# Wide matmuls on a constant ahead of, and between, the first matmuls of an attention stage

## Chip, cores and metric

The kernel runs on one core of one Trainium2 chip. The metric is the device time of one execution in microseconds; the time before is the median of three runs. The profile is one further execution of the same kernel on the same core.

## The reference, cut to what matters

Two transformer layers over T = 1024 tokens of width C = 512, each an attention followed by a feed-forward part, with residuals and a layer norm behind each. Both attentions have 32 heads of width 16 over all 1024 tokens and are causal.

```python
q, k = rope(q), rope(k)
scores = einsum('bhqd,bhkd->bhqk', q, k) / sqrt(16)
attn = softmax(where(causal, scores, -inf))
y = einsum('bhqk,bhkd->bhqd', attn, v)
```

Layer 0 has a small adapter attention over ten extra tokens besides, then a lookup part as feed-forward. Layer 1 has eight key and value heads, each shared by four query heads, and a SwiGLU feed-forward. The change touches only the attention stage, which both layers run.

## The kernel before, in words

The stages follow one another with a barrier between them: projection of layer 0, adapter, attention 0, its finish, lookup, projection of layer 1, attention 1, its finish, SwiGLU. `attention(nc, layer, ...)` is built once for each layer.

An attention stage works in 16 units `u`: eight head groups `g` (four heads each) for the lower 512 queries (`c` = 0), then the same eight groups for the upper 512 queries (`c` = 1). I call the first eight the narrow units and the last eight the wide ones. A narrow unit has 4 key tiles `kt` of 128 keys, a wide one has 8.

For each unit the kernel does two things.

- *Maxima.* The row maxima of the scores must be known before the exponentials. `entry(number, b, what)` multiplies queries by keys (line 849, `q_st` as weights, 48 rows), adds the causal mask on the diagonal block with two bf16 matmuls on constants (lines 855 and 857, `picks` and `maskb`), and VectorE reduces the result (line 973). A narrow unit has 12 such entries, a wide one 28, and one more entry "T" (line 837) transposes the previous unit's maxima. Entries go round a ring of three PSUM banks (`RING`), so TensorE is at most three entries ahead of VectorE. GpSimd splits the maxima in two parts (lines 998 and 1000), VectorE joins their halves in wide units (line 948) and copies their transpose out of PSUM (line 964), and four small DMAs (line 810) write them as two extra rows into `q_st`.
- *Attention proper.* `scores(u, kt, p)` (line 872) computes transposed scores with the maximum already subtracted through the extra rows; it waits for those DMAs at the unit's first key tile and for the exponential two steps back. ScalarE takes the exponential (line 926), GpSimd masks the diagonal tile (line 1013), `values(u, kt)` (line 891) multiplies by the values into PSUM bank 6, and ScalarE copies the finished unit out (line 934).

The order on TensorE is written out by hand. First the entries of units 0 and 1 with nothing between them, then the two first `scores`, then the loop over units: in unit `u` the key tiles' `scores` and `values` are interleaved with the entries of unit `u + 2`, spread evenly over the unit's slots. So units 0 to 5 carry the entries of narrow units, units 6 and 7 carry the entries of wide units, units 8 to 13 are wide with wide entries, and units 14 and 15 have none. The last instruction of a unit shows in the trace as the copy of line 934, which ScalarE issues behind the second exponential of the next unit.

The DMA queue in layer 0 holds, when the stage begins, the loads of the first four units' queries and keys and behind them the 2 MB load of `x_tok` (line 602, issued in the adapter stage). In layer 1 only the first unit is loaded before the stage; units 1 to 3 are issued at its start.

The constant `picks[0]` is the 128x128 bf16 tile that the mask matmuls of line 855 also read. Bank 6 is not used before the first `values`, which starts a new accumulation.

Of the kernel before, what the change touches and what calls it, by code (L numbers as in the profile page):

```python
# [32 lines left out]
P = 128  # L33
# [705 lines left out]
def attention(nc, layer, phase, stacked, arena_o, arena_p, v_tok, v_grp, ident, picks, maskb, psum):  # L739
# [18 lines left out]
    def key_pair(p):  # L758
        return p if layer == 0 else 0
# [26 lines left out]
    def first_column(c, kt):  # L786

        return max(0, P * kt - 512 * c)

    with phase as ph, ExitStack() as own:  # L790
# [37 lines left out]
        def _(pe):  # L828
            def entry(number, b, what):

                if number >= len(RING):
                    pe.wait_ge(qk_taken, number - len(RING) + 1)
                bank = RING[number % len(RING)]
                if what == "T":
                    u = b - 1
                    pe.wait_ge(max_ready, u + 1)
                    pe.transpose(psum[0:2 * R * 4, bank, 0:P],
                                 mst[:, u % 2, :, :].bitcast(F32).rearrange("p j i -> p (j i)"), ident[:, :])\
                        .then_inc(qk_ready, 1)
                    return  # L840
                i, heads, kc, width = what
                s, c = b % NS, steps[b][0]
                if number == first_entry[b]:
                    pe.wait_ge(q_loaded[s], 32 * (b // NS + 1))
                    pe.wait_ge(k_loaded[s], 32 * (b // NS + 1))
                for n, r in enumerate(heads):
                    p, rows = r // 2, slice(64 * (r % 2), 64 * (r % 2) + KS)
                    end = width * (n + 1)
                    last = pe.matmul(psum[:, bank, width * n:end],  # L849
                                     q_st[rows, s, p, P * i:P * i + P],  # L850
                                     k_st[rows, s, key_pair(p), 512 * kc:512 * kc + width],
                                     start=True, stop=kc < c)
                    if kc == c:
                        half = slice(64 * (r % 2), 64 * (r % 2) + 64)
                        pe.matmul(psum[:, bank, end - P:end], picks[0][half, :], maskb[half, :],  # L855
                                  start=False, stop=False)
                        last = pe.matmul(psum[:, bank, end - 64:end], picks[1][half, :],  # L857
                                         maskb[half, 0:64], start=False, stop=True)
                last.then_inc(qk_ready, 1)

            def scores(u, kt, p):

                s, c = u % NS, steps[u][0]
                n = first_exp[u] + 2 * kt + p
                o = first_column(c, kt)
                if kt == 0 and p == 0:
                    pe.wait_ge(max_loaded[s], 64 * (u // NS + 1))
                if n >= 2:
                    pe.wait_ge(exp_ready, n - 1)
                for t in range(2):  # L870
                    rows = slice(64 * t, 64 * t + KM)
                    last = pe.matmul(psum[:, 2 * (n % 2) + t, o:512],  # L872
                                     k_st[rows, s, key_pair(p), P * kt:P * kt + P],
                                     q_st[rows, s, p, o:512], start=True, stop=True)
                last.then_inc(scores_ready, 1)

            def values(u, kt):
# [16 lines left out]
                                     start=kt == 0, stop=kt == 4 * c + 3, tile_position=(0, 32 * r))  # L894
                last.then_inc(pv_done, 2)

            for b in range(2):
                for n, what in enumerate(lists[b]):
                    entry(first_entry[b] + n, b, what)
            scores(0, 0, 0)  # L900
            scores(0, 0, 1)
            for u in range(NU):
# [878 lines left out]
```

## Time and profile before

| what | us |
|---|---|
| median of 3 runs | 1122.52 |
| the runs | 1118.2, 1122.52, 1139.11 |
| the profiled execution, device time | 1121.8 |
| its span, first to last instruction | 1119.9 |
| mean granted TensorE clock | 0.815 of full speed |

The span is what the trace covers; some 1.9 us of the device time lie around it. Granted clock 1.00 is 2.4 GHz and 0.50 is 1.2 GHz. In tables of stretches each engine's busy time is followed by the number of instructions in brackets, and PEclk is the mean granted clock in the stretch. Matmuls overlap, so TensorE can be "busy" all the time and still be waiting now and then.

### The profile page before, as it was taken

Reading aid. Unit: us, or ns where it says so; the run is one execution under the profiler, and the core shown is the slowest. Engines: PE = TensorE matmul, PEld = TensorE weight load, DVE = VectorE, ACT = ScalarE, POOL = GpSimd, SP = SyncE. Lnnn points to the kernel's source line nnn. Section 1 sums busy time; section 2 is a strip of 40 time slices with the busy share of each in tenths; the row PEclk is TensorE's granted clock in tenths of the full one; section 3 lists DMA queues with packets and bytes.
Section 4 is the critical chain, followed back from the end, with each engine's and each line's share of the span. In section 5 each row is a group of like instructions: output and inputs, shape, how many; then the busy total and the mean of one; then the engine's idle time right before and its main releaser. Section 6 shows DMA issues by size and latency. Waiting matters only on the chain. (4 is left out here: it accounts for less than half of the span.)

```text
span 1119.9 us, 15914 instructions
## 1 busy us (share of the span) xinstructions
PE 1007.8 (90%) x5974; PEld 620.4 (55%) x5974; DVE 643.8 (57%) x1151; ACT 486.3 (43%) x750; POOL 228.5 (20%) x457
## 2 busy tenths in 40 slices
PE   7787998999999999798777799999999988889998
PEld 4455874555544543484354555555445435767766
DVE  6441543455778884384844444567888833835464
ACT  4220323342267676522632133422666774346740
POOL 3222002222111212106132022211111123012300
PEclk9995975555589998997879655555899999989999
DMA  9553081222221200200015511211112001051101
GB/s 306 168 176 118 1 181 41 60 74 53 70 53 48 69 22 2 94 1 1 0 55 182 171 23 45 52 42 48 31 30 59 3 2 38 1 176 57 38 20 57
DMA packets 39774, 74.75 MB, mean 67 GB/s; under 512 B 6512, under 2 KB 8368, under 8 KB 39696
## 3 DMA queue, kind: packets, MB, share of 16 engines
q1 hardware_dynamic: 39696, 73.70, 22.5%
q8 instruction: 50, 0.82, 0.3%
q14 instruction: 28, 0.23, 0.1%
HBM read 50.29 MB, written 22.87 MB: 65 GB/s over the span
## 5 line engine op out<-in xcount | busy, mean ns | idle before, releaser
L973 DVE TENSOR_REDUCE mx<-psum 128x1 f32<-128x512 f32 (+3 forms) x640 | 373.0, 631 | 163.0 <-PE psum L857 139.4
L926 ACT ACTIVATE arena_p<-psum 128x1024 f32<-128x1024 f32 (+3 forms) x384 | 292.8, 809 | 301.6 <-PE psum L872 299.8
L849 PE MATMUL psum<-k_st,q_st 48*128 48x512 f32 (+3 forms) x768 | 312.1, 505 | 10.6 <-PEq L242 4.0
L849 PEld LDWEIGHTS psum<-k_st,q_st 48*128 48x128 f32 x768 | 168.9, 246 | 141.4 <-DVE mx L973 120.9
L872 PE MATMUL psum<-q_st,k_st 50*128 50x512 f32 (+3 forms) x768 | 227.0, 479 | 8.7 <-ACT arena_p L926 5.6
L891 PE MATMUL psum<-arena_p,v_grp 128*32 128x512 f32 (+3 forms) x1536 | 203.3, 609 | 9.9 <-POOL arena_p L1013 8.8
L1013 POOL TENSOR_SCALAR_AFFINE_SELECT arena_p<-arena_p 128x256 f32<-128x256 f32 x256 | 101.2, 409 | 295.9 <-ACT arena_p L926 290.5
L872 PEld LDWEIGHTS psum<-q_st,k_st 50*128 50x128 f32 x768 | 127.9, 233 | 48.2 <-ACT arena_p L926 37.2
L855 PE MATMUL psum<-maskb,pick 64*128 64x128 bf16 x512 | 132.8, 289 | 0.0
L857 PE MATMUL psum<-maskb,pick_high 64*128 64x64 bf16 x512 | 109.1, 231 | 0.0
L257 PE MATMUL psum<-x_h,w 128*128 128x512 f32 x224 | 89.2, 462 | 10.6 <-DVE w L482 7.4
L855 PEld LDWEIGHTS psum<-maskb,pick 64*128 64x128 bf16 x512 | 60.7, 124 | 32.1 <-issue 21.8
L857 PEld LDWEIGHTS psum<-maskb,pick_high 64*128 64x128 bf16 x512 | 61.7, 126 | 0.0
L257 PEld LDWEIGHTS psum<-x_h,w 128*128 128x128 f32 x224 | 45.3, 202 | 27.8 <-issue 9.6
L891 PEld LDWEIGHTS psum<-arena_p,v_grp 128*32 128x32 f32 x1536 | 33.2, 119 | 47.3 <-POOL arena_p L1013 20.1
L440 ACT CAST arena_p<-arena_o 128x512 fp32r<-128x512 f32 x26 | 16.1, 619 | 93.9 <-DMA q_parts<-arena_p 50.4
L556 POOL TENSOR_TENSOR arena_o<-arena_o 128x512 f32<-128x512 f32 x26 | 35.3, 1358 | 100.2 <-DVE arena_o L498 100.2
L390 PE MATMUL psum<-arena_o,arena_f 128*128 128x512 f32 x52 | 31.6, 692 | 22.1 <-ACT arena_o L458 22.0
L476 DVE TENSOR_TENSOR arena_p<-arena_o,arena_p 128x512 fp32r<-128x512 f32 x26 | 19.0, 730 | 50.8 <-ACT arena_p L440 50.8
L1567 PE MATMUL psum<-x_h,ff_w 128*128 128x512 f32 (+1 forms) x176 | 45.7, 403 | 1.6 <-ACT ff_flags L1624 0.9
L257 PE MATMUL psum<-x_l,w 128*128 128x512 f32 x112 | 46.4, 414 | 0.0
L998 POOL CAST mst<-mx 128x16 fp32r<-128x16 f32 x32 | 6.3, 198 | 194.7 <-DVE mx L973 97.7
(200 smaller groups left out, 1153.8 us busy)
## 6 DMA issues: line engine op xcount, KB each, us to landing
q_parts<-arena_p SPq DMA_DIRECT2D x48, 256.0 KB
q_st<-q_parts SPq DMA_DIRECT2D x64, 192.0 KB, 4.0
k_parts<-arena_p SPq DMA_DIRECT2D x30, 256.0 KB
k_st<-k_parts SPq DMA_DIRECT2D x32, 200.0 KB
k_st<-k_parts SPq DMA_DIRECT2D x16, 400.0 KB
ff_raw<-in_w_in SPq DMA_DIRECT2D x11, 512.0 KB, 3.5
arena_w<-in_w SPq DMA_DIRECT2D x12, 256.0 KB, 5.7
ff_wd_raw<-in_w_down SPq DMA_DIRECT2D x1, 2560.0 KB, 11.8
```

The costliest lines, as they stand in the source:

```text
L257: last = pe.matmul(out, lhs[i](k), rhs[j](k), start=k + n == 0, stop=k == KC - 1 and n == 2)
L390: pe.matmul(psum[:, 2 + n % 2, :], rot, raw[:, n % 2, :], start=True, stop=True)\
L556: pool.tensor_tensor(rotated(n), t_cos[:, s, :], t_sin[:, s, :], ALU.add)\
L849: last = pe.matmul(psum[:, bank, width * n:end], q_st[rows, s, p, P * i:P * i + P], k_st[rows, s, key_pair(p), 512 * kc:512 * kc + width], ...
L855: pe.matmul(psum[:, bank, end - P:end], picks[0][half, :], maskb[half, :], start=False, stop=False)
L857: last = pe.matmul(psum[:, bank, end - 64:end], picks[1][half, :], maskb[half, 0:64], start=False, stop=True)
L872: last = pe.matmul(psum[:, 2 * (n % 2) + t, o:512], k_st[rows, s, key_pair(p), P * kt:P * kt + P], q_st[rows, s, p, o:512], start=True, st ...
L891: last = pe.matmul(psum[32 * r:32 * r + VW, 6, o:512], v_grp[:, u % 2, kt, r if layer == 0 else 0, :], pr[:, (n + r // 2) % NP_RING, r % 2 ...
L926: act.activation(pr[:, n % NP_RING, :, o:512], psum[:, 2 * (n % 2):2 * (n % 2) + 2, o:512], ACT.Exp, scale=scale).then_inc(exp_ready, 1)
L973: dve.tensor_reduce(mx[:, b % 2, kc, col:col + 4 * len(heads) - 3:4], src, AX, ALU.max)\
L1013: pool.affine_select(out=tri, in_=tri, compare_op=ALU.is_ge, fill=0.0, base=0, pattern=[[0, 2], [1, P]], channel_multiplier=-1).then_inc(m ...
L1567: last = pe.matmul(psum[0:rows[i], 2 * (n % 3) + u, :], ff.w_hl[a][:, i % 2, col:col + rows[i]], x_hl[b][:, k, 512 * c:512 * c + 512], sta ...
```

## The change

A helper issues `count` matmuls of 512 columns on the constant tile, whose result is never read. It is called with 18 ahead of the first entry of the stage, and with 1 behind each of the 25 entries of units 0 and 1. As `attention` runs twice, this adds 86 matmuls. Nothing is removed, and no wait is added.

```diff
+            def spin(count):
+
+                for _ in range(count):
+                    pe.matmul(psum[:, 6, :], picks[0][:, :],
+                              picks[0][:, :].rearrange("p (o n) -> p o n", o=1).broadcast_to([P, 4, P]),
+                              start=True, stop=True)
+
+            spin(18)
             for b in range(2):
                 for n, what in enumerate(lists[b]):
                     entry(first_entry[b] + n, b, what)
+                    spin(1)
             scores(0, 0, 0)
             scores(0, 0, 1)
             for u in range(NU):
```

## Rows read from the trace of the kernel before

**Rows 1.** The page's span in 40 slices: TensorE's busy tenths and granted clock.

```profile
PE   7787998999999999798777799999999988889998
PEclk9995975555589998997879655555899999989999
```

**Rows 2.** Stretches: us, busy us (instructions) of PE, PEld, DVE, ACT, POOL; PEclk, DMA, GB/s.

```profile
172.00:264.00 92.00, 87.20 (x582) 51.93 (x583) 43.07 (x77) 35.53 (x56) 22.18 (x63) 0.50 0.23 58
264.00:311.00 47.00, 45.55 (x231) 24.80 (x230) 33.13 (x60) 12.52 (x19) 7.89 (x22) 0.50 0.24 62
333.00:431.00 98.00, 94.24 (x804) 47.57 (x801) 82.38 (x150) 66.60 (x85) 20.96 (x55) 1.00 0.17 45
650.00:742.00 92.00, 88.27 (x588) 52.59 (x586) 45.18 (x81) 35.66 (x56) 21.63 (x66) 0.50 0.19 46
```

**Rows 3.** Timeline of ScalarE: ends of units 0, 5, 7, 8, 9 of layer 0.

```profile
187.03 0.59 ACT L934 COPY arena_o<-psum 128x512 f32<-128x512 f32 x1
...
263.66 0.59 ACT L934 COPY arena_o<-psum 128x512 f32<-128x512 f32 x1
...
310.06 0.59 ACT L934 COPY arena_o<-psum 128x512 f32<-128x512 f32 x1 [1.69 <-PE psum L891]
332.17 0.59 ACT L934 COPY arena_o<-psum 128x512 f32<-128x512 f32 x1
351.91 0.59 ACT L934 COPY arena_o<-psum 128x512 f32<-128x512 f32 x1
```

**Rows 4.** The same in layer 1: ends of units 0 and 5.

```profile
663.44 0.59 ACT L934 COPY arena_o<-psum 128x512 f32<-128x512 f32 x1
...
739.24 0.59 ACT L934 COPY arena_o<-psum 128x512 f32<-128x512 f32 x1
```

**Rows 5.** Timeline: wide matmuls (512 columns) at either clock, outside attention.

```profile
569.27 0.77 PE L257 MATMUL psum<-x_h,w 128*128 128x512 f32 x1 [3.17 <-PEq L242]
...
571.54 1.05 PE L257 MATMUL psum<-x_h,w 128*128 128x512 f32 x2
...
572.82 1.05 PE L257 MATMUL psum<-x_h,w 128*128 128x512 f32 x2
...
995.50 1.98 PE L1567 MATMUL psum<-x_l,ff_w 128*128 128x512 f32 x8
997.31 1.98 PE L1567 MATMUL psum<-x_h,ff_w 128*128 128x512 f32 x8
```

**Rows 6.** Timeline of TensorE at the start of attention 0.

```profile
151.88 0.29 PE L849 MATMUL psum<-k_st,q_st 48*128 48x128 f32 x1 [1.08 <-PEq L242]
...
166.98 0.26 PE L857 MATMUL psum<-maskb,pick_high 64*128 64x64 bf16 x1
170.31 1.22 PE L872 MATMUL psum<-q_st,k_st 50*128 50x512 f32 x4 [3.08 <-DMA q_st<-mT]
```

**Rows 7.** Timeline of all engines at the start of attention 1.

```profile
638.81 0.44 PE L849 MATMUL psum<-k_st,q_st 48*128 48x128 f32 x1 [2.66 <-DMA k_st<-k_parts]
...
646.04 0.77 PE L872 MATMUL psum<-q_st,k_st 50*128 50x512 f32 x1
...
647.55 3.53 ACT L926 ACTIVATE arena_p<-psum 128x1024 f32<-128x1024 f32 x4 [17.23 <-PE psum L872]
...
648.63 0.69 PE L872 MATMUL psum<-q_st,k_st 50*128 50x384 f32 x2 [0.69 <-ACT arena_p L926]
```

**Rows 8.** Stretches, columns as in rows 2: where the granted clock moved or held.

```profile
150.00:152.00 2.00, 0.92 (x9) 0.76 (x7) 0.00 (x0) 1.03 (x2) 0.28 (x1) 1.00 1.10 174
152.00:168.00 16.00, 14.97 (x97) 10.22 (x97) 13.50 (x25) 0.00 (x0) 0.88 (x4) 0.50 0.91 213
428.00:432.00 4.00, 3.44 (x35) 1.96 (x27) 3.97 (x7) 2.94 (x4) 0.00 (x0) 1.00 0.00 0
432.00:436.00 4.00, 3.11 (x13) 0.81 (x15) 0.45 (x2) 1.52 (x2) 0.97 (x3) 0.50 0.01 2
904.00:908.00 4.00, 2.54 (x23) 1.28 (x21) 3.09 (x6) 3.39 (x4) 0.65 (x3) 1.00 0.00 0
```

## Prediction

> **What bounds the kernel now.** I read the span in 40 slices first, the clock line above all. The granted clock is near 1 almost everywhere, but in two runs of slices, one in each layer, it stands at 5 while TensorE's digits are 9 [rows 1]. The reader is to see that these are the first halves of the two attention stages.
>
> The stretches say it in numbers. In the narrow units of layer 0 (172 to 264 us) the clock is 0.50, which is the 1.2 GHz level, and TensorE is busy 87.20 of 92 us while VectorE has 43.07. In the wide units (333 to 431 us) the clock is 1.00, the 2.4 GHz level, and VectorE has 82.38 of 98 us [rows 2]. So narrow units are bound by a slow TensorE, and wide ones by VectorE with its waits. The ends of the units give the price: units 1 to 5 take (263.66 − 187.03) / 5 = 15.33 us each, the mixed units 6 and 7 take 46.40 together, unit 8, in which the clock rises, 22.11, and a wide unit at full clock (351.91 − 332.17) 19.74 [rows 3]. In layer 1 a narrow unit takes (739.24 − 663.44) / 5 = 15.16 us [rows 4].
>
> The change does nothing for the computation. Its only possible gain is that the added matmuls lift the clock before the narrow units begin and that it then stays up. So there are two questions: what the narrow units would take at 1.00, and whether the clock survives until they run.
>
> **Term 1, the 18 matmuls ahead of each stage.** A 512-column matmul costs 0.427 us at the low clock (three between 571.54 and 572.82) and (997.31 − 995.50) / 8 = 0.226 us at the high one [rows 5]. The clock falls as the stage opens: 1.00 in the two microseconds before it, with a gap of 1.08 us ahead of the first entry, 0.50 behind it [rows 6, 8]. Bounds are 18 x 0.226 = 4.1 us and 18 x 0.427 = 7.7 us. I take 6 us: where a row of wide matmuls lifted the clock elsewhere, it had run from 569.27 to about 575.3 at half speed [rows 5], which here would leave four matmuls at full speed, 14 x 0.427 + 4 x 0.226 = 6.9 us; starting while the clock is still up gives 4.1, and 6 lies between, nearer to the row.
>
> Not all of this reaches the end. In attention 0 TensorE has finished all entries at 167.0 and then waits 3.08 us for the maxima's DMA, which lands behind the x_tok load; scores start at 170.31 [rows 6]. With entries 6 us later they end at 173.0, the wait is gone (the small DMAs then meet an emptier queue), and scores start 2.7 us later than now. In attention 1 TensorE waits 2.66 us for the second unit's keys until 638.81, so it is done with the first 12 entries at 636.15 [rows 7]. 6 us later that is 642.15, and 3.3 us are added. Together +6 us; with 4.1 us of spins it is +2.2 (0.8 and 1.4), with 7.7 it is +9.4.
>
> **Term 2, one matmul beside each of 25 entries.** 25 x 0.226 = 5.7 us of TensorE work per stage at full clock. VectorE needs 13.50 us for these entries in a stretch of 16 us [rows 8], and TensorE's own work for them halves from 14.97 us, to 7.5; 7.5 + 5.7 = 13.2 us is still under VectorE's. Cost: nothing, hidden under the reduces. At the low clock the cover is gone: 25 x 0.427 = 10.7 us on top of 14.97 (a rival below).
>
> **Term 3, narrow units at full clock.** No row shows one. Lower bound: half of 15.33, 7.7 us, if TensorE remains the only limit. Upper bound: a wide unit's pace per key tile, 19.74 / 8 = 2.47, times 4 = 9.9 us, although its key tiles carry more columns. Between them I use VectorE: 43.07 / 92 x 15.33 = 7.2 us of work per narrow unit, and a wide unit at full clock keeps VectorE busy 82.38 / 98 = 0.84 of its time [rows 2, 3]. 7.2 / 0.84 = 8.5 us. Layer 1: 45.18 / 92 x 15.16 = 7.45, over 0.84, 8.9 us [rows 2, 4]. That saves 6.8 and 6.3 us per unit, for six units (unit 0 starts and ends like the others) 40.7 and 37.8 us.
>
> Mixed units: 33.13 / 47 of 46.4 / 2 = 23.2 us is 16.4 us of VectorE work [rows 2], over 0.84, 19.5 us. Two save 46.4 − 38.9 = 7.5 us; unit 8 saves 22.1 − 19.7 = 2.4 us. A stage that keeps its clock thus gains about 50.6 us in layer 0 and, by the same working with about 2 us less for its last three units, 47 in layer 1. The late thing is then VectorE, as in the wide units. Behind the mixed units nothing changes.
>
> **Does the clock survive the start of unit 0?** This decides. While the entries run with a wide matmul beside each, TensorE is well occupied and I expect 1.00. Then the extra matmuls end. Unit 0 opens with score matmuls, and its first four exponentials run back to back for 3.53 us; from the third score group on, TensorE waits for an exponential each time. At half speed the first four score matmuls last 1.22 us [rows 6] and the next groups 0.69 us each [rows 7]; halved, and with a second such group, that is 0.6 + 0.35 + 0.35 = 1.3 us in the first 3.5, to which two small entries add some 0.6 (estimate: four matmuls like the one at 151.88, 0.29 us, halved, is 0.58 [rows 6]). The first values come only behind the masks. TensorE is then occupied about 1.9 of 3.5 us, 54%, where it was almost fully so before.
>
> Compare stretches at full clock. From 904 to 908 TensorE was busy 2.54 of 4 us, 63%, and the clock held. From 150 to 152 it was busy 0.92 of 2, with an idle stretch of 1.08, and the clock fell; and 428 to 432, busy 3.44 of 4 us, was followed by 4 us at 0.50 [rows 8, 6]. The start of unit 0 is thinner than the one stretch and no worse than the others, so neither outcome is excluded, and losing is the likelier for a single stage. Once lost there, the clock does not return: 92 us of narrow units with TensorE busy 0.95 of the time never raised it [rows 2]. So each stage is a draw, which depends on how the instants at which the clock is set fall against this thin stretch, and it can differ from execution to execution. I give a stage something over four chances in ten.
>
> The Trainium skill, "TensorE: Matmul & The Clock Gate", section "Part 1: The HAM clock gate", tells it more simply: the clock is low by default, sustained activity releases it, idleness brings it back. Read by that, busy narrow units should have been released in the kernel before; this trace disagrees (0.50 at 87.20 busy of 92 us). By the same rule, with no really long idle stretch in the new order, both stages would be kept, which gives the 1030 us of the second case below.
>
> **Cases and their times**, from the profiled 1121.8 us (0.7 under the median of 1122.52, so I let it stand for it):
>
> - *One stage keeps the clock, the other loses it*: 1121.8 + 6 − 49 = 1078.8 us, own range 1069 to 1089 (the bounds of a narrow unit, 7.7 to 9.9, move six units by −6 and +7, the spins by ±4). For it: each stage is its own draw, and a median over executions favours the middle. Chance 0.38.
> - *Both keep it*: 1121.8 + 6 − 97.6 = 1030 us (1016 to 1046). For it: 1.46 us without a matmul between 904 and 908 did not cost the clock [rows 8]. Against it: the thin start. Chance 0.23.
> - *The lift works but both stages lose the clock at the first scores*: only the 6 us remain, 1128 us (1124 to 1132). This is the change that does not do what it says. Chance 0.32.
> - *Slower*: the 18 matmuls do not lift the clock, or it falls among the entries, and 18 + 25 matmuls a stage run at the low one: 7.7 + 10.7 = 18.4 us of TensorE work, on the path since TensorE leads there at the low clock. Attention 0 starts its scores at 167.0 + 18.4 = 185.4 instead of 170.3 (+15.1), attention 1 pays 18.4 less its wait of 2.66 us (+15.7). That is 1153 us. It decides if the clock in the entries' stretch reads 0.50. Against it: wide matmuls lifted the clock within about 6 us in the row named. Chance 0.07.
>
> **Numbers.** The likeliest is the first, 1079 us. The range reaches from the second case's low end to the third's high end, 1016 to 1133 us; the slow case and the tails are left out. About 2% is what a measurement tells from no change here. Faster by more (under 1100): 0.38 + 0.23, 0.61. Within 2%: 0.32. Slower: 0.07.
>
> **What would show it.** The first entry of each stage moves 4 to 8 us behind the first wide matmul. The clock line reads 1.00 while the entries run, and VectorE's reduces there follow one another as now. The wait for the maxima's DMA at attention 0 shrinks from 3.08 us to under 1. In a stage that keeps its clock the copies of line 934 come 8 to 10 us apart and the mixed units take 19 to 20; in one that loses it the clock drops within some 4 us of the first scores, and the copies stay 15.2 to 15.3 us apart. It is wrong if the clock drops later, inside the narrow units (then steady narrow work is too thin for it even at full speed), or if the units at 1.00 take over 10 us.

## The result and the profile after

| | kernel before | kernel changed |
|---|---|---|
| median, us | 1130.82 (4 runs, 1118.2 to 1150.35) | 1159.51 (4 runs, 1150.38 to 1172.86) |
| the profiled execution, us | 1121.8 | 1172.86 |
| its mean granted clock | 0.815 | 0.799 |

The ratio is 1.032, with a 95% interval from 1.016 to 1.048: slower, where I had forecast faster; whether by more than 2% the interval leaves open. The kernel before has one execution more here than ahead of the prediction, the one of 1150.35. Ratios here leave out executions more than 1.5% above the fastest of their kernel, so they can differ a little from a quotient of medians. Line numbers behind 897 are 9 higher than before.

The page's 40 slices, which answer to [rows 1]:

```profile
PE   7778999999999998889696999999999998979998
PEclk9996975555589998998799655555589989989999
```

Both attention stages still show five slices at half clock. The high clock did not carry into the narrow units. The timeline of ScalarE, ends of units 0 and 5 of layer 0 and of units 7 and 8 of layer 1, answers to [rows 3, 4]:

```profile
205.42 0.59 ACT L943 COPY arena_o<-psum 128x512 f32<-128x512 f32 x1
...
282.02 0.59 ACT L943 COPY arena_o<-psum 128x512 f32<-128x512 f32 x1
...
820.97 0.58 ACT L943 COPY arena_o<-psum 128x512 f32<-128x512 f32 x1 [1.70 <-PE psum L891]
852.96 0.59 ACT L943 COPY arena_o<-psum 128x512 f32<-128x512 f32 x1
```

A narrow unit takes (282.02 − 205.42) / 5 = 15.32 us, as before. But unit 0 of layer 0 ends 18.4 us later than the 187.03 of [rows 3]. So the loss lies ahead of the units, and the timeline of TensorE from the stage's start to the first scores shows it (answering to [rows 6, 7]):

```profile
150.95 4.04 PE L900 MATMUL psum<-pick 128*128 128x512 bf16 x18 [0.93 <-PEq L242]
154.93 0.32 PE L849 MATMUL psum<-k_st,q_st 48*128 48x128 f32 x1
...
188.70 1.22 PE L872 MATMUL psum<-q_st,k_st 50*128 50x512 f32 x4
...
643.46 5.64 PE L900 MATMUL psum<-pick 128*128 128x512 bf16 x18 [2.62 <-PEq L242]
...
682.23 1.22 PE L872 MATMUL psum<-q_st,k_st 50*128 50x512 f32 x4
```

From first entry to first scores layer 0 takes 188.70 − 154.93 = 33.8 us, where it took 170.31 − 151.88 = 18.4 before [rows 6]. The stretches say how, the entries at the high clock first and then at the low one, in each layer (columns as in [rows 2]; they answer to [rows 8]):

```profile
155.50:158.50 3.00, 3.00 (x23) 1.92 (x21) 1.55 (x3) 0.00 (x0) 0.00 (x0) 1.00 1.06 200
158.60:188.00 29.40, 29.40 (x94) 13.07 (x94) 12.51 (x21) 0.00 (x0) 0.42 (x2) 0.50 0.22 68
650.00:653.50 3.50, 3.50 (x26) 2.24 (x25) 1.98 (x4) 0.00 (x0) 0.00 (x0) 1.00 0.93 218
653.60:682.00 28.40, 28.40 (x91) 12.62 (x90) 11.96 (x21) 0.00 (x0) 0.42 (x2) 0.50 0.09 23
```

Two things are to be seen. The 18 matmuls did their part: the clock reads 1.00 as the entries begin. In layer 0 they held it, for it had not fallen yet; in layer 1 they lifted it, from 0.50 at 643.3 to 1.00 at 646.7. And while it is 1.00, TensorE is busy in all of 3.00 us and VectorE in 1.55, where before VectorE had 13.50 of 16 us [rows 8]. TensorE leads even at full clock. Then, at 158.6 and at 653.6, in the middle of the entries, the clock falls, and 29.4 and 28.4 us follow at half speed.

**The balance of the profiled execution.** It is the slowest of the four, 1172.86 us. Scores of layer 0 start 188.70 − 170.31 = 18.4 us later. The end of unit 15 is 18.0 later, and 3.8 us are regained before the next attention, whose first instruction is 643.46 − 629.22 = 14.2 later. Its scores are 682.23 − 646.04 = 36.2 later, so this stage adds 22.0 us. In unit 8 the clock rises again in the kernel before (at 790.3, 4.8 us into the unit); here it came back only at 858.3, in unit 9, and unit 8 took 852.96 − 820.97 = 31.99 us against 21.68 before, +10.3. What is left is +2.8 in the other units, 2.1 of it in unit 9, and +1.65 behind the stage. The sum: 18.4 − 0.4 − 3.8 + 22.0 + 10.3 + 2.8 + 1.7 = 51.0, the difference of the spans. The 10.3 is taken as a draw, not as the change: the experiments below show the same 31.98 or 31.99 us in unit 8 of one layer or the other, in kernels with quite other starts. It may also account for much of the spread of the kernel before; that was not traced.

### The profile page after: what moved, and what is told of

Its sections match the earlier page's. It is cut to its first block and busy times, and to the rows that moved or that the text cites. A ratio compares the mean times of both kernels' runs of the same rounds, so it can differ in the third digit from the quotient of the medians.

```text
span 1170.9 us, 16086 instructions
## 1 busy us (share of the span) xinstructions
PE 1068.9 (91%) x6060; PEld 643.2 (55%) x6060; DVE 649.4 (55%) x1151; ACT 486.3 (42%) x750; POOL 228.9 (20%) x457
## 5 line engine op out<-in xcount | busy, mean ns | idle before, releaser
L849 PE MATMUL psum<-k_st,q_st 48*128 48x512 f32 (+3 forms) x768 | 326.9, 512 | 3.5 <-DVE mx L982 2.2
L849 PEld LDWEIGHTS psum<-k_st,q_st 48*128 48x128 f32 x768 | 174.0, 250 | 153.3 <-DVE mx L982 118.6
L872 PE MATMUL psum<-q_st,k_st 50*128 50x512 f32 (+3 forms) x768 | 232.5, 491 | 5.6 <-ACT arena_p L935 5.5
L891 PE MATMUL psum<-arena_p,v_grp 128*32 128x512 f32 (+3 forms) x1536 | 209.7, 627 | 9.7 <-POOL arena_p L1022 8.6
L872 PEld LDWEIGHTS psum<-q_st,k_st 50*128 50x128 f32 x768 | 130.9, 241 | 46.1 <-ACT arena_p L935 36.5
L855 PE MATMUL psum<-maskb,pick 64*128 64x128 bf16 x512 | 136.0, 290 | 0.0
L891 PEld LDWEIGHTS psum<-arena_p,v_grp 128*32 128x32 f32 x1536 | 33.6, 120 | 49.3 <-POOL arena_p L1022 19.5
```

The source lines that it names most:

```text
L849: last = pe.matmul(psum[:, bank, width * n:end], q_st[rows, s, p, P * i:P * i + P], k_st[rows, s, key_pair(p), 512 * kc:512 * kc + width], ...
L872: last = pe.matmul(psum[:, 2 * (n % 2) + t, o:512], k_st[rows, s, key_pair(p), P * kt:P * kt + P], q_st[rows, s, p, o:512], start=True, st ...
L891: last = pe.matmul(psum[32 * r:32 * r + VW, 6, o:512], v_grp[:, u % 2, kt, r if layer == 0 else 0, :], pr[:, (n + r // 2) % NP_RING, r % 2 ...
```

## The experiments

The theory after the result: a 128-row wide matmul does not run beside an entry but between entries, so it costs its whole length; the stage loses there, and the clock is lost as well. The rivals: the 18 ahead are what costs; the loss is only that of a low clock; or narrow units would not be faster at full clock anyway.

**Each part alone.** `ahead_only` keeps the 18 and drops the ones beside:

```diff
-                    spin(1)
```

> Only the 18 matmuls ahead of each stage; none beside the entries. Theory 'serial' (the matmul beside each entry uses all 128 rows, so it can run neither beside the entry before it nor beside the one behind it, and that is what costs): the entries go back to one per 0.6 us, unit 0's first scores come 2 to 4 us later than in the kernel before in each stage, and the time is 2 to 10 us over the kernel before. Rival 'ahead' (the matmuls ahead, and the moment they put the stage at, cost most): 25 us or more over the kernel before, as the changed kernel. Both expect 0.50 in the narrow units, since the clock falls among the entries or at the first scores.

Measured: 1121.18 us (1119.37 to 1132.27), ratio 1.004 (0.997 to 1.011): no change. Clock 1.00 to 159.0, then 0.50. First scores at 169.15.

`beside_only` drops the 18:

```diff
-            spin(18)
```

> Only the one matmul beside each of 25 entries; none ahead. Theory 'serial': the entries take 1.34 to 1.45 us each at the low clock, first scores of attention 0 at about 151.9 + 36 = 187 us instead of 170, of attention 1 about 18 us later than before within the stage; total 28 to 36 us over the kernel before. Rival 'ahead': under 15 us over it.

Measured: median 1169.42 us (1155.49 to 1183.52), ratio 1.034 (1.031 to 1.036). The clock is 0.50 from 151.5 on. So the whole loss comes with the 25 matmuls beside the entries of each stage, and the 18 ahead are next to free: in layer 0 their 4.04 us vanish in the wait for the maxima's DMA [rows 6]. I had forecast that most of them would; in `ahead_only` the first scores even come 1.2 us earlier than before.

**Beside, but in another shape.** `beside_half` keeps 18 and 25, but the one beside an entry uses only the 64 rows of the array that the entry has just used, and writes to bank 2 or 3:

```diff
-            def spin(count):
+            def spin(count, beside=None):
...
+                side = 0 if beside in (None, "T") else beside[1][0] % 2
+                rows = slice(0, P) if beside is None else slice(64 * side, 64 * side + 64)
...
-                    pe.matmul(psum[:, 6, :], picks[0][:, :],
-                              picks[0][:, :].rearrange("p (o n) -> p o n", o=1).broadcast_to([P, 4, P]),
+                    pe.matmul(psum[:, 6 if beside is None else 2 + side, :], picks[0][rows, :],
+                              picks[0][rows, :].rearrange("p (o n) -> p o n", o=1).broadcast_to([rows.stop - rows.start, 4, P]),
...
-                    spin(1)
+                    spin(1, what)
```

> As the changed kernel, but each matmul beside an entry uses 64 rows, those of the half that the entry just used, and goes to bank 2 or 3; its 512 columns stay. Theory 'serial': the next entry, on the other half in most cases, can run beside it again, so an entry comes every 0.6 to 1.0 us instead of 1.34 to 1.45 at the low clock, and the time is 5 to 18 us over the kernel before. Rival (the 512 columns themselves take the time on the array, rows or not): entries stay at 1.3 us or more, and the time stays 30 us over.

Measured: 1127.73 us (1123.35 to 1131.62), ratio 1.008 (1.003 to 1.012). As many added matmuls of the same 512 columns, and three quarters of the loss is gone. An entry comes in two kinds: for the first two query tiles it holds two heads, for the others one, and the times differ. Entries at full clock in either kernel, from the timeline of all engines. First the changed kernel, the wide matmuls ahead of and behind a two-head entry of layer 0, and the same for a one-head entry of layer 1:

```profile
157.49 0.39 PE L900 MATMUL psum<-pick 128*128 128x512 bf16 x1
...
158.53 0.56 PE L900 MATMUL psum<-pick 128*128 128x512 bf16 x1
...
652.64 0.39 PE L900 MATMUL psum<-pick 128*128 128x512 bf16 x1
...
652.96 0.18 PEld L849 LDWEIGHTS psum<-k_st,q_st 48*128 48x128 f32 x1 [0.23 <-issue]
652.96 0.44 PE L849 MATMUL psum<-k_st,q_st 48*128 48x384 f32 x1
...
653.43 0.53 PE L900 MATMUL psum<-pick 128*128 128x512 bf16 x1
```

Then `beside_half`, a one-head entry of the same width:

```profile
163.84 0.38 PE L902 MATMUL psum<-pick 64*128 64x512 bf16 x1
163.92 0.18 PEld L849 LDWEIGHTS psum<-k_st,q_st 48*128 48x128 f32 x1
163.93 0.44 PE L849 MATMUL psum<-k_st,q_st 48*128 48x384 f32 x1
...
164.30 0.38 PE L902 MATMUL psum<-pick 64*128 64x512 bf16 x1
164.39 0.18 PEld L849 LDWEIGHTS psum<-k_st,q_st 48*128 48x128 f32 x1
164.39 0.49 PE L849 MATMUL psum<-k_st,q_st 48*128 48x512 f32 x1
```

With 128 rows the next entry's weights are loaded only at 652.96, when the wide matmul that began at 652.64 is nearly through, and wide matmuls are 653.43 − 652.64 = 0.79 us apart (1.04 us around the two-head entry). With 64 rows the next entry begins 0.09 us behind the start of the wide matmul and runs beside it, and the pair takes 164.30 − 163.84 = 0.46 us. Entries use alternate halves of the rows; in these rows a matmul over all of them overlaps with neither neighbour. The variant changes the bank as well as the rows; no entry uses bank 6, 2 or 3, so the rows are the likelier cause, but the bank was not varied alone. `ahead_only`, with nothing beside, has six reduces from 155.5 to 158.5, where the changed kernel has three.

The clock also lasted longer in `beside_half`, to 167.4 in layer 0, through all entries. This is its stretch of entries:

```profile
153.80:167.30 13.50, 12.48 (x119) 8.47 (x116) 12.40 (x25) 0.00 (x0) 0.42 (x2) 1.00 0.77 204
```

VectorE leads again (12.40 of 13.50 us). From first entry to first scores it took 168.10 − 153.28 = 14.8 us, against 18.4 before. The clock fell in a wait of 1.36 us for the maxima's DMA, just ahead of these scores, and in layer 1 at 648.8, behind them: in effect the third of my cases.

**More of it.** Is the loss the low clock alone? `beside_three` puts three beside each entry instead of one, enough that the clock stays up:

```diff
-                    spin(1)
+                    spin(3)
```

> The changed kernel with three wide matmuls beside each entry instead of one. Theory 'serial': at the high clock an entry came every 1.04 us, at the low one every 1.4, and two more add 0.45 us each time; with TensorE better filled the clock stays 1.00 among the entries, which come every 1.45 to 1.55 us, and unit 0's first scores of attention 0 come 18 to 22 us later than before, after which the clock falls as in the changed kernel. Rival (the clock falls among any serialised entries): it falls within the first entries, which then take 2.2 us each, and the scores come some 40 us later.

Measured in a single run: 1163.97 us. The clock is 1.00 through all entries of both layers; this is layer 0:

```profile
156.00:188.00 32.00, 32.00 (x173) 14.51 (x172) 14.51 (x25) 0.00 (x0) 0.42 (x2) 1.00 0.35 91
```

First scores come at 188.19, 17.9 us later than before, at full clock. So fillers that do not overlap cost time at full clock too. How much of the changed kernel's loss is that? Entries come 1.22 to 1.47 us apart here, 32.1 us from first entry (156.09) to first scores, and a filler more or less is (0.82 − 0.39) / 2 = 0.215 us, since three in a row show 0.82 us and one 0.39. With one filler instead of three that is 32.1 − 50 x 0.215 = 21.3 us (an estimate). Had the clock held, the changed kernel's first scores would thus have come at 154.93 + 21.3 = 176.2, about 6 us later than before; the other 12 of its 18.4 us come with the low clock. The low clock without the fillers costs nothing here, as `ahead_only` shows, which lost it at 159.0. It takes both. The clock of `beside_three` was lost behind the entries: at 190.8, just behind the first scores, and in layer 1 at 709.6, as unit 0 ends.

**Fillers where TensorE has time.** `blocks` gives the same kind of matmul in blocks of four behind every third entry, four behind the two first scores, and 4, 2 and 2 in the first slots of unit 0:

```diff
+                    if (first_entry[b] + n) % 3 == 2:
+                        spin(4)
             scores(0, 0, 1)
+            spin(4)
...
+                    if u == 0 and slot < 3:
+                        spin((4, 2, 2)[slot])
```

> 18 ahead; then four wide matmuls behind every third entry instead of one behind each; four behind the two first scores, and four, two and two in unit 0's first three slots, where TensorE waits for exponentials. Theory 'a narrow unit holds a clock that it is given': the clock reads 1.00 from the stage's start through the narrow units, these take 8.5 to 8.9 us each and the mixed ones about 19.5, and the time is 1015 to 1045 us. Rival 'narrow work is too thin even at full speed': the clock drops within the narrow units, which then take 15.3 us, and the time is within 15 us of the kernel before. Second rival (the lift is lost among the entries again): the same time, with 0.50 already before the first scores.

Measured: 1125.18 us (1100.7 to 1133.09) against 1120.64 for the kernel before beside it, no difference that four such runs can tell. This is the time of the rival "narrow work is too thin even at full speed", though `blocks_pool` below speaks against that rival. The clock stayed 1.00 to 181.5 in layer 0 and to 659.4 in layer 1, past entries and unit 0, and from first entry to first scores it took 166.06 − 149.60 = 16.5 us, against 18.4 before [rows 6] and 33.8 in the changed kernel. A block of four takes 1.04 us and comes every third entry, while VectorE still has entries in the ring of banks to reduce. But then the clock went within unit 1, and the timelines of GpSimd and TensorE show the wait that was not in my prediction:

```profile
180.76 0.20 POOL L1011 CAST mst<-mx 128x16 fp32r<-128x16 f32 x1 [3.65 <-DVE mx L986]
181.04 0.22 POOL L1013 TENSOR_TENSOR mst<-mx,mst 128x16 fp32r<-128x16 f32 x1
181.21 0.40 POOL L997 COPY v_grp<-v_tok 128x256 f32<-128x256 f32 x1
181.56 1.48 POOL L1026 TENSOR_SCALAR_AFFINE_SELECT arena_p<-arena_p 128x256 f32<-128x256 f32 x4
182.38 1.93 PE L891 MATMUL psum<-arena_p,v_grp 128*32 128x512 f32 x8 [1.42 <-POOL arena_p L1026]
```

GpSimd stands 3.65 us waiting for the last reduce of the maxima it is to split, with four masks queued behind, and `values` wait for those masks, 1.42 us; the clock falls at 181.5, in this wait.

**The queue of GpSimd.** `blocks_pool` is `blocks` with the split and the value load of the next unit moved: in a narrow unit behind its second and fourth mask instead of ahead of the masks.

```diff
+                if c == 1 and u + 1 < NU:
+                    split_max(u + 1)
+                    load_v(u + 1)
...
+                    if c == 0 and u and b == 2:
+                        split_max(u + 1)
+                    if c == 0 and u and b == 4:
+                        load_v(u + 1)
...
-                if u + 2 < NU:
-                    split_max(u + 2)
-                    load_v(u + 2)
```

> As 'blocks', and GpSimd's order changed: the split of the maxima and the copy of the values for the next unit stand behind the first two (and four) masks of a narrow unit instead of ahead of them. Theory 'new wait': in 'blocks' the clock fell at 181.5 and 659.4 us because at full clock the first masks of unit 1 wait behind the split, which waits for VectorE's last maximum, so that TensorE stands idle 1.42 us ahead of unit 1's values. With the order changed this gap goes, the clock stays at 1.00 through the narrow units of both stages, these take 8 to 9 us each, and the time is 1020 to 1050 us. Rival 'narrow work is too thin': the clock falls within units 1 to 3 all the same, and the time stays within 20 us of the kernel before.

Measured: median 1053.28 us (1051.61, 1053.14, 1053.42, and one of 1099.82), ratio 0.940 (0.935 to 0.945), which is that of the first three. It beats both kernels, though in the fourth execution the kernel before by only 2%; that one was not traced. The timeline of ScalarE, ends of units 0, 1, 4 and 5 of layer 0:

```profile
181.48 0.59 ACT L947 COPY arena_o<-psum 128x512 f32<-128x512 f32 x1
190.50 0.59 ACT L947 COPY arena_o<-psum 128x512 f32<-128x512 f32 x1
...
217.56 0.59 ACT L947 COPY arena_o<-psum 128x512 f32<-128x512 f32 x1
227.42 0.59 ACT L947 COPY arena_o<-psum 128x512 f32<-128x512 f32 x1
```

Stretches in the narrow units of both layers:

```profile
172.00:217.00 45.00, 44.92 (x480) 26.72 (x478) 32.82 (x63) 26.40 (x43) 17.83 (x50) 1.00 0.33 83
628.00:672.00 44.00, 43.53 (x472) 26.14 (x464) 32.90 (x64) 27.00 (x43) 18.15 (x53) 1.00 0.31 75
```

A narrow unit at 1.00 takes (217.56 − 181.48) / 4 = 9.02 us in place of 15.33. VectorE is busy 32.82 / 45 = 0.73 of it. Units 1 to 5 take 45.9 us in place of 76.6 [rows 3], and 45.5 in place of 75.8 in layer 1 [rows 4]: 61 of the 68.4 us between the two profiled executions (1121.8 − 1053.42).

`pool_only` is that order of GpSimd without any filler (the diff above alone):

> The kernel before with GpSimd's order changed as in 'blocks_pool' and no added matmul. Both theories: the clock is 0.50 in the narrow units as before; a TensorE gap of 0.9 us ahead of each narrow unit's first values goes, so 0 to 12 us under the kernel before. If it alone gives as much as 'blocks_pool', the added matmuls do nothing.

Measured over ten runs: 1113.81 us (1109.47 to 1115.95), ratio 0.994 (0.991 to 0.997). A small gain of its own: a narrow unit takes 14.38 us, still at the low clock. So nearly all of the 6% comes only with both together.

**Is each piece needed?** `entries_fed` is `blocks_pool` without the fillers behind the first scores and in unit 0:

```diff
-            spin(4)
...
-                    if u == 0 and slot < 3:
-                        spin((4, 2, 2)[slot])
```

> As 'blocks_pool' without the wide matmuls behind the first scores and in unit 0's slots: 18 ahead and four behind every third entry remain. The step of the prediction 'the start of unit 0 is too thin': the clock falls within some 4 us of the first scores in most executions, narrow units then take 14.4 us, and most times are 1100 to 1120 us. Rival (the thin start is bridged, only the units' own gaps mattered): the clock holds as in 'blocks_pool' and the time is its own less the few us of the left-out matmuls, 1048 to 1054 us.

Measured: 1052.24, 1072.86, 1094.08 and 1103.96 us. In the profiled one the clock fell at 175.5 in layer 0 and held in layer 1 until 714.8, with units of 14.4 and of 9.0 us:

```profile
171.35 0.50 PE L872 MATMUL psum<-q_st,k_st 50*128 50x512 f32 x1
...
173.37 0.44 PE L872 MATMUL psum<-q_st,k_st 50*128 50x384 f32 x2 [0.88 <-ACT arena_p L936]
...
174.28 0.44 PE L872 MATMUL psum<-q_st,k_st 50*128 50x384 f32 x2 [0.47 <-ACT arena_p L936]
```

These are the score groups of layer 0 that wait for the exponentials, just ahead of the fall. This is the draw of my prediction, seen stage by stage. One good execution in four, where `blocks_pool` has three, hints that the fillers in unit 0 help; so few runs do not prove it.

`no_ahead` and `eight_ahead` are `blocks_pool` with 0 and 8 ahead instead of 18:

```diff
-            spin(18)
+            spin(0)
```

> As 'blocks_pool' without the 18 matmuls ahead of the stage. If the lift ahead is needed: the clock falls as the stage opens (as in the kernel before, at 152.1 and 629.9 us), four wide matmuls behind every third entry at the low clock take 1.7 us and make the entries slower, and the time is 1100 us or more unless the blocks lift the clock by themselves. Rival (the blocks of four alone lift it within a few us): the time is that of 'blocks_pool' less up to 8 us, 1044 to 1053 us.

> As 'blocks_pool' with 8 matmuls ahead instead of 18: 2.2 us less at the high clock per stage. If the clock is reached as safely: 1047 to 1053 us. If 8 are too few in a stage that opens at the low clock: 1075 us or more in some executions.

Measured: without any, 1074.73, 1092.57, 1093.91 and 1168.56 us; in the last, which is the profiled one, the clock of layer 0 fell at 150.8 and came back only in the wide units, and a block of four took 1.89 us instead of 1.04, with first scores at 177.47. With 8, six runs from 1057.6 to 1130.88 us, median 1077.37; the ratio of 0.959 (0.950 to 0.967) is that of the two quickest. The 18 are not needed in every execution, but the runs with fewer scatter, and none is below the three good ones with 18.

**Two attempts to do better.** `blocks_fed` also puts a wide matmul ahead of two of the twelve entries of units 2 to 7, into the entry's own bank:

```diff
+                if 2 <= b < 8 and i in (2, 3) and heads[0] == 0:
+                    pe.matmul(psum[:, bank, :], picks[0][:, :],
...
```

> As 'blocks_pool', and in units 0 to 5 two of the twelve entries get one wide matmul each, into the entry's own bank ahead of its own matmuls (0.23 us plus some 0.3 us of lost overlap, so about 1 us per unit). Theory 'new wait': not needed, so the same clock and 5 to 12 us slower than 'blocks_pool'. Rival 'narrow work is too thin': this one keeps the clock where 'blocks_pool' loses it, and is the faster of the two by 30 us or more.

Measured: 1064.18 us (1058.73 to 1114.18), ratio 0.950 (0.943 to 0.957). The narrow unit takes 9.5 us instead of 9.02, 0.24 us for each of the two fillers: their own length, and not the 0.3 us of lost overlap that I had allowed besides.

`mixed_fed` tries to hold the clock through the mixed units instead, with one ahead of every third entry of units 7 to 9:

```diff
+                if b in (7, 8, 9) and number % 3 == 0:
+                    pe.matmul(psum[:, bank, :], picks[0][:, :],
...
```

> As 'blocks_pool', and every third entry of units 7, 8 and 9 gets one wide matmul into its own bank ahead of its own (the entries that are issued in unit 5 and in the mixed units 6 and 7, where 'blocks_pool' loses the clock at 226.5 and 673.6 us). Theory 'thin': TensorE has too little to do there at full speed, since VectorE sets the pace; fed, the clock stays, the two mixed units take 19 to 20 us each instead of 22.4 and 23.7, and 10 to 18 us are gained on 'blocks_pool': 1036 to 1044 us. Rival 'late DMA': the clock falls at unit 6's wait for its maxima's DMA (0.86 us), fed or not, and the time is that of 'blocks_pool' or up to 10 us more.

Measured: 1079.27 us (1075.02 to 1083.7), ratio 0.964 (0.959 to 0.970), slower than `blocks_pool`. The clock was lost all the same, at 240.6 and 687.8, and units 6 and 7 of layer 0 took 23.4 and 28.2 us. What takes the clock there stays open. In `blocks_pool` it fell at 226.5, behind this row, a wait for the DMA that writes the maxima:

```profile
225.05 0.50 PE L872 MATMUL psum<-q_st,k_st 50*128 50x512 f32 x2 [0.86 <-DMA q_st<-mT]
```

Whether this wait or the thin work around it is the cause was not separated.

## Why the prediction was wrong, point by point

**Term 1, the 18 ahead: right.** 4.04 us where they began at the high clock and 5.64 where they began at the low one, against bounds of 4.1 and 7.7, and the clock read 1.00 behind them in both stages. `ahead_only` shows that they cost about nothing in the end (ratio 1.004, interval 0.997 to 1.011).

**Term 2, one beside each entry: here the prediction failed.** The step was "7.5 + 5.7 = 13.2 us is still under VectorE's. Cost: nothing, hidden under the reduces". It adds busy times of matmuls as if they were all that TensorE needs. But the 7.5 us hold for entries that overlap on alternate halves of the rows and load weights ahead. A matmul over all 128 rows ends both overlaps: an entry with its wide matmul takes 0.79 us with one head and 1.04 us with two at full clock, against VectorE's 13.50 / 25 = 0.54 us [rows 8]. So 25 of them take some 21 us even at the high clock (the estimate from `beside_three`), not 13.2, and 33.8 us as measured, most of it at the low one. `beside_half` (0.46 us for the pair, +0.8%) and `beside_three` (17.9 us lost at a clock of 1.00) show it from both sides. I never asked what shape the added matmul had against its neighbours.

**The clock among the entries: wrong too.** "While the entries run with a wide matmul beside each, TensorE is well occupied and I expect 1.00." It was occupied, 3.00 of 3.00 us, and the clock fell. By the estimate above this is the larger part of the loss, some 12 of the 18.4 us in layer 0. The changed kernel lost the clock at 158.6; `ahead_only`, with nothing beside, at 159.0; `beside_half`, which kept the pace, at 167.4; `beside_three` at 190.8. So it is not the serialising alone that loses it; what does stays open, for no experiment varies it alone. The Trainium skill, "TensorE: Matmul & The Clock Gate", section "Part 1: The HAM clock gate", has the clock released by sustained activity. This trace disagrees more sharply than that of the kernel before: 29.40 busy of 29.40 us at 0.50.

**Which case came.** The slow rival, to which I had given 0.07. It was placed "among the entries", with +15.1 and +15.7 us; measured were +18.4 and +22.0. Its test, the clock in the entries' stretch, reads 1.00 for some 4 us and then 0.50. Its price was 25 x 0.427 = 10.7 us of added work at the low clock, a sum of busy times again; an entry with its wide matmul really takes 1.34 to 1.45 us there with one head and 1.58 to 1.79 with two, at least 0.8 more than VectorE's pace. The chance was too small because its reason "against" spoke only of the lift by the 18, and nothing in the profile supported the entries' holding it. That the price came out near is in part luck: it adds up the wrong thing.

**Term 3, narrow units at full clock: right,** though it was not reached by the change. Predicted 8.5 and 8.9 us within 7.7 to 9.9, measured 9.02 in `blocks_pool`, once GpSimd's order is changed. VectorE's busy share is 0.73 there and not 0.84; its work per unit, 32.82 / 45 x 9.02 = 6.6 us, is under the 7.2 I took. What was missing is that at full clock another wait comes forward, GpSimd's split ahead of the masks. With it in place (`blocks`) the clock fell in unit 1 in the profiled execution; what a narrow unit at 1.00 takes in the kernel's own order of GpSimd was never measured. The mixed units, for which I had 19.5 us, take 22.4 and 23.7 in `blocks_pool`, since the clock is lost there.

**The start of unit 0: right, as far as four runs tell.** Without fillers there it is a draw (`entries_fed`), and what is lost there does not come back in narrow units.

## What to carry to other kernels

A filler matmul among other matmuls is only free if it overlaps with its neighbours as the work does: compare its rows of the array with theirs, and measure the distance from one to the next, not the sum of busy times. Where the work overlaps by halves of the array, put fillers in blocks where the engine waits anyway, or give them only the rows that were just used. When a bound engine is made twice as fast, read the other engines' queues for what is late next; here moving GpSimd's split and value load was worth 0.6% alone, the blocks of fillers alone nothing that could be measured, and both together 6% in three executions of four.

## What the runs showed of the hardware

- TensorE can be busy without a gap at granted clock 0.50 for 29.4 us, and the clock can fall from 1.00 in a stretch in which it is busy 3.00 of 3.00 us.
- A bf16 matmul of 512 columns shows 0.38 to 0.39 us at full clock whether it has 128 or 64 rows; with 64 rows the next entry on the other half starts 0.09 us behind it, with 128 rows 0.32 us behind it (652.64 to 652.96).
- Unit 8, in which the clock comes back in most traces, takes 21.1 to 22.4 us there, and 31.98 to 31.99 us where the clock comes back only in unit 9: in layer 1 of the changed kernel and in layer 0 of `ahead_only` and of `entries_fed`. That this is why one program differs by 10 us and more from one execution to the next is likely, but no program was traced twice.
